# Attention heads of two kinds: one after the other, or in alternating pieces of two tiles

## The reference

```python
xn  = layernorm(x)
# attention 1 ("poly"): 16 heads of 128, rope on q and k
s   = (q1 @ k1.T) ** 4 * causal
o1  = (s @ v1) / max(s.sum(-1), 1e-6);  attn1 = o1 @ Wo1.T
# attention 2 ("sfmx"): 16 heads of 128 on h1 = rmsnorm(xn)
p   = softmax(causal(q2 @ k2.T / sqrt(128)))
attn2 = (p @ v2) @ Wo2.T;   mod = 0.1 * tanh(attn2 @ A)
# MLP on h = rmsnorm(xn)
g   = silu(h @ W_in.T + mod * (h @ A) @ B);  up = h @ W_up.T
out = x + attn1 + xn + (g * up) @ W_down.T
```

## Time and profile before

| | us |
|---|---|
| median of the runs (2: 8290.56 and 8651.73) | 8471.14 |
| the profiled execution | 7604.0 |
| its span, first to last instruction, slowest core | 7602.5 |
| spans of all cores | 7588.0 to 7602.5 |
| mean granted TensorE clock, all cores | 0.895 to 0.897 of full speed |

### The profile page before, as it was taken

One profiled execution on the slowest core, in us unless ns is written; L12 is line 12 of the kernel. 1 busy time (PEld: TensorE's weight loads), 2 busy tenths in 40 slices (PEclk: granted clock), 3 DMA queues, 4 the chain that ended last, 5 costly groups with the idle time before them and its releaser, 6 DMA issues.

```text
span 7602.5 us, 67624 instructions; the slowest of 8 cores (7588.0 to 7602.5 us)
## 1 busy us (share of the span) xinstructions
PE 5990.3 (79%) x25648; PEld 2466.4 (32%) x25648; DVE 1493.0 (20%) x1800; ACT 1372.8 (18%) x1974; POOL 823.5 (11%) x877
## 2 busy tenths in 40 slices
PE   3188885998666666666678858999999999679779
PEld 0033342444212121121223313444444444234334
DVE  3333302000223323233221121000000000111112
ACT  1011112111345454454520011000000000000000
POOL 0000000000242333424310000000000000000000
PEclk6699997999888887887789979999999999789889
DMA  4322232433101000010023141132231230686775
GB/s 84 122 64 61 61 61 39 77 75 63 43 25 34 25 25 25 26 34 25 25 48 96 25 86 45 34 67 55 46 67 42 59 67 12 176 216 189 201 193 186
DMA packets 285258, 552.72 MB, mean 73 GB/s; under 512 B 143879, under 2 KB 177031, under 8 KB 277511
## 3 DMA queue, kind: packets, MB, share of 16 engines
q0 software_dynamic: 60432, 310.72, 19.5%
q1 hardware_dynamic: 206078, 204.11, 8.5%
q10 hardware_dynamic: 18432, 33.56, 1.7%
HBM read 598.98 MB, written 125.85 MB: 95 GB/s over the span
## 4 chain that ended last, share of the span: by engine, by line
PE 70%; ACT 9%; DVE 8%; DMA 5%; issue 4%; POOL 3%; DVEq 1%; ACTq 0%; POOLq 0%; SPq 0%
PE big L360 18%; PE big L752 12%; PE big L826 12%; PE big L757 12%; PE big L612 6%; ACT px L543 4%; POOL px L538 3%; PE big L563 3%; PE big L568 3%; DMA pb<-gu_sp 2%; DVE px L553 2%; PE big L527 2%; DMA px<-xt 2%; ACT px L365 2%; PE big L762 1%
## 5 line engine op out<-in xcount | busy, mean ns | idle before, releaser
L752 PE MATMUL big<-pb 128*128 128x512 bf16 x4096 | 1556.8, 380 | 6.2 <-DVE px L725 6.2
L757 PE MATMUL big<-pb 128*128 128x512 bf16 x4096 | 1553.9, 379 | 0.0
L360 PE MATMUL big<-pb,px 128*128 128x512 bf16 x6144 | 1341.2, 380 | 260.2 <-DMA px<-ropes 185.8
L826 PE MATMUL big<-pb 128*128 128x512 bf16 x4096 | 892.8, 381 | 202.4 <-DMA pb<-gu_sp 202.4
L563 PE MATMUL big<-px 128*128 128x512 bf16 x1280 | 570.3, 446 | 568.9 <-DVE px L553 290.9
L360 PEld LDWEIGHTS big<-pb,px 128*128 128x128 bf16 x6144 | 600.9, 98 | 984.7 <-issue 270.2
L538 POOL TENSOR_TENSOR px<-px 128x512 bf16<-128x512 f32 x640 | 662.7, 1058 | 1238.8 <-ACT px L534 1163.4
L826 PEld LDWEIGHTS big<-pb 128*128 128x128 bf16 x4096 | 402.4, 98 | 693.9 <-issue 216.1
L568 PE MATMUL big<-px,ones 128*128 128x512 bf16 x1280 | 573.4, 448 | 0.0
L752 PEld LDWEIGHTS big<-pb 128*128 128x128 bf16 x4096 | 400.6, 98 | 519.1 <-issue 66.8
L757 PEld LDWEIGHTS big<-pb 128*128 128x128 bf16 x4096 | 401.4, 98 | 454.0 <-issue 1.6
(11 more groups left out here) (97 smaller groups left out, 2184.2 us busy)
## 6 DMA issues: line engine op xcount, KB each, us to landing
pb<-gu_sp POOLq DMA_DIRECT2D x32, 4096.0 KB, 19.6
pb<-wint POOLq DMA_DIRECT2D x16, 2048.0 KB, 15.9
pb<-wupt POOLq DMA_DIRECT2D x16, 2048.0 KB, 26.3
gu_sp<-px SPq DMA_DIRECT2D x64, 512.0 KB
pb<-wdnt POOLq DMA_DIRECT2D x8, 4096.0 KB, 29.9
px<-xt SPq DMA_DIRECT2D x32, 512.0 KB
q_sp<-px SPq DMA_DIRECT2D x32, 512.0 KB
k_sp<-px SPq DMA_DIRECT2D x32, 512.0 KB
```

The source lines that it names most:

```text
L360: e.matmul(PS(4 * bi + tb), wbuf[b][:, jc * 128:(jc + 1) * 128], src_pool[:, jc * NT + tb * 512: jc * NT + (tb + 1) * 512], start=(jc == 0 ...
L752: e.matmul(PS(gbk), winb[:, jc * FB + fc * 128: jc * FB + (fc + 1) * 128], PB1[:, jc * NT + tb * 512: jc * NT + (tb + 1) * 512], start=(jc ...
L757: e.matmul(PS(ubk), wupb[:, jc * FB + fc * 128: jc * FB + (fc + 1) * 128], PB1[:, jc * NT + tb * 512: jc * NT + (tb + 1) * 512], start=(jc ...
L826: e.matmul(PS(bk), PB2[:, fc * ICB + ici * 128: fc * ICB + (ici + 1) * 128], PB1[:, fc * 512:(fc + 1) * 512], start=(fc == 0), stop=last),
```

## The change

`attention_head` becomes a generator. Its first argument after the head is `sid`, 0 for poly and 1 for sfmx. It yields after its loads, after the norms of k, after those of q, after the bias, after every second tile (and the last, incomplete pair of the pipeline), and after each block's scaling. The loop over heads makes both generators and calls them in turn until both end, poly first. So on every engine pieces of the poly head stand between pieces of the sfmx head.

With it go: each kind has its own accumulator banks (4 and 5, or 6 and 7) for all blocks, its own two of the four score slots, and its own single `arm1` buffer. Within an iteration SV(t-2) and DN(t-2) now come ahead of QK(t). The norms use banks 6 and 7 in place of 4 and 5.

In the last stage `e1` and `e2` have one buffer each in place of two, and a DVE drain follows the sum.

```diff
-        def attention_head(kind, h, sh, q_sp, k_sp, v_sp, outF, bar):
-            b = sh % 2
-            w0 = list(bar) if sh < 2 else []
+        def attention_head(kind, h, sid, q_sp, k_sp, v_sp, outF, bar):
+            b = sid
+            w0 = list(bar)
+            sv_bk = 4 + 2 * sid
+            dn_bk = 5 + 2 * sid
...
+            yield
             t_negb = None
             if kind == "sfmx":
...
+                S.tc[("nsq",)] = tr
+                yield
+                tsq2 = S.op("dve", lambda e, b=b: e.tensor_tensor(out=aqsq[:], in0=aqh[b][:], in1=aqh[b][:],
+                                                                  op=ALU.mult),
+                            waits=[tq, tm], incs=[("dve", 1)])
...
+                S.tc[("aqsqpe",)] = tm
+                yield
...
+                yield
             for tqb in range(NTB):
-                sv_bk = 4 + 2 * (tqb % 2)
-                dn_bk = 5 + 2 * (tqb % 2)
                 for t_ in range(ntile + 2):
+                    if t_ >= 2:
+                        tt_ = t_ - 2
+                        sl2 = 2 * sid + tt_ % 2
...
                     if t_ < ntile:
-                        sl = t_ % 4
+                        sl = 2 * sid + t_ % 2
...
-                    if t_ >= 2:
-                        tt_ = t_ - 2
-                        sl2 = tt_ % 4
...
-                ab = (2 * sh + tqb) % 2
-                arm1 = arm1s[ab]
+                    if t_ % 2 == 1:
+                        yield
+                arm1 = arm1s[sid]
...
+                yield
...
         for h in range(H):
-            attention_head("poly", h, 2 * h, scr["q1_sp"], scr["k1_sp"], scr["v1_sp"], PB1, bar_p2a)
-            attention_head("sfmx", h, 2 * h + 1, scr["q2_sp"], scr["k2_sp"], scr["v2_sp"], PB2, bar_p2a)
+            bar_h = bar_p2a if h == 0 else []
+            ga = attention_head("poly", h, 0, scr["q1_sp"], scr["k1_sp"], scr["v1_sp"], PB1, bar_h)
+            gb = attention_head("sfmx", h, 1, scr["q2_sp"], scr["k2_sp"], scr["v2_sp"], PB2, bar_h)
+            a_done = b_done = False
+            while not (a_done and b_done):
+                if not a_done:
+                    try:
+                        next(ga)
+                    except StopIteration:
+                        a_done = True
...
-        e1s = [pxf(40, 512), pxf(0, 512)]
-        e2s = [pxf(42, 512), pxf(2, 512)]
+        e1 = pxf(40, 512)
+        e2 = pxf(42, 512)
...
+                               waits=[tlx, t_ar, t_mr, S.tc.get(("e1",))], incs=[("dve", 1)])
...
+                    S.op("dve", lambda e: e.drain())
+                    S.tc[("e2",)] = teo
...
-                    S.tc[("e1", eb)] = tst
+                    S.tc[("e1",)] = tst
```

More of the change, by code:

```diff
@@ new lines, in attention_head @@
+                tsq = S.op("dve", lambda e, b=b: e.tensor_tensor(out=aqsq[:], in0=akh[b][:], in1=akh[b][:],
+                                                                 op=ALU.mult),
+                           waits=[tk, S.tc.get(("aqsq",)), S.tc.get(("aqsqpe",))] + w0,
+                           incs=[("dve", 1)])
+                for qtr in range(NTB):
+                    nbk = sv_bk + qtr % 2
+                    tm = S.op("pe", lambda e, qtr=qtr, nbk=nbk: e.matmul(
+                              PS(nbk), ones128[:], aqsq[:, qtr * 512:(qtr + 1) * 512],
+                              start=True, stop=True),
+                              waits=[tsq, S.t_ps[nbk]], incs=[("pe", 1)])
+                    tr = S.op("dve", lambda e, qtr=qtr, nbk=nbk: e.reduce_max(
+                              out=nmax8[:, qtr:qtr + 1],
+                              in_=PS(nbk), axis=mybir.AxisListType.X),
+                              waits=[tm], incs=[("dve", 1)])
+                    set_ps([nbk], tr)
@@ new lines, in attention_head @@
+                S.tc[("nsq",)] = tr
+                yield
+                tsq2 = S.op("dve", lambda e, b=b: e.tensor_tensor(out=aqsq[:], in0=aqh[b][:], in1=aqh[b][:],
+                                                                  op=ALU.mult),
+                            waits=[tq, tm], incs=[("dve", 1)])
+                for qtr in range(NTB):
+                    nbk = sv_bk + qtr % 2
+                    tm = S.op("pe", lambda e, qtr=qtr, nbk=nbk: e.matmul(
+                              PS(nbk), ones128[:], aqsq[:, qtr * 512:(qtr + 1) * 512],
+                              start=True, stop=True),
+                              waits=[tsq2, S.t_ps[nbk]], incs=[("pe", 1)])
+                    tr = S.op("dve", lambda e, qtr=qtr, nbk=nbk: e.reduce_max(
+                              out=nmax8[:, 4 + qtr:4 + qtr + 1],
+                              in_=PS(nbk), axis=mybir.AxisListType.X),
+                              waits=[tm], incs=[("dve", 1)])
+                    set_ps([nbk], tr)
@@ L523, in attention_head @@
                 for t_ in range(ntile + 2):
+                    if t_ >= 2:
+                        tt_ = t_ - 2
+                        sl2 = 2 * sid + tt_ % 2
+                        S.op("pe", lambda e, sl2=sl2, tt_=tt_, b=b, sv_bk=sv_bk,
+                             st=(tt_ == 0), en=(tt_ == ntile - 1):
+                             e.matmul(PS(sv_bk), avh[b][:, tt_ * 128:(tt_ + 1) * 128],
+                                      as4[sl2][:], start=st, stop=en),
+                             waits=[t_w[tt_], tv] + ([S.t_ps[sv_bk]] if tt_ == 0 else []))
+                        tsv = S.op("pe", lambda e, sl2=sl2, tt_=tt_, dn_bk=dn_bk,
+                                   st=(tt_ == 0), en=(tt_ == ntile - 1):
+                                   e.matmul(PS(dn_bk), ones128[:], as4[sl2][:], start=st, stop=en),
+                                   waits=[S.t_ps[dn_bk]] if tt_ == 0 else [],
+                                   incs=[("pe", 1)])
+                        S.tc[("as4", sl2)] = tsv
                     if t_ < ntile:
-                        sl = t_ % 4
+                        sl = 2 * sid + t_ % 2
                         tqk = S.op("pe", lambda e, sl=sl, t_=t_, tqb=tqb, b=b:
@@ L583, in attention_head @@
                                out=arm1[:], in_=PS(dn_bk), func=AF.Ln),
-                               waits=[tsv, S.tc.get(("arm", ab))], incs=[("act", 1)])
+                               waits=[tsv, S.tc.get(("arm", sid))], incs=[("act", 1)])
                     set_ps([dn_bk], tln)
@@ L647, in build @@
         for h in range(H):
-            attention_head("poly", h, 2 * h, scr["q1_sp"], scr["k1_sp"], scr["v1_sp"], PB1, bar_p2a)
-            attention_head("sfmx", h, 2 * h + 1, scr["q2_sp"], scr["k2_sp"], scr["v2_sp"], PB2, bar_p2a)
+            bar_h = bar_p2a if h == 0 else []
[8 more added lines that the diff above has]
+                        a_done = True
+                if not b_done:
+                    try:
+                        next(gb)
+                    except StopIteration:
+                        b_done = True
         bar_attn = S.barrier()
@@ L861, in build @@
                     set_ps([bk], te2)
                     S.op("dve", lambda e: e.drain())
[L863 to L864 removed]
+                    teo = S.op("dve", lambda e: e.tensor_tensor(out=e1[:], in0=e1[:], in1=e2[:], op=ALU.add),
                                incs=[("dve", 1)])
[L866 removed]
```

37 lines of the change are left out of this document (8 added, 29 removed).

## The result

The changed kernel is faster: the ratio to the kernel before is 0.972, with a 95% interval from 0.967 to 0.977. Forecast was a ratio of 0.977 and, for an execution like the profiled one, 7429 us; the comparable executions of the changed kernel took 7417 to 7439 us, beside 7604 and 7665 before. The forecast of the median in absolute terms, 8276 us with a range from 8060 to 8600, was wrong: the median of 13 runs is 7650 us (7417 to 8336), and that of 10 runs of the kernel before is 8136 (7604 to 8652).

The account below looks back on a forecast made before the run. The attention stage was taken as bound by waits. A pair's terms, 33.9 + 51.2 + 15.3 + 6.3 + 1.9, made 108.6 us; 7604 - 178 + 3 = 7429 us, scaled to 8276 us, range 8060 to 8600.

Parts of the forecast that it names:

- The start-up: Start of each pair of heads, from the last sfmx scaling through loads, norms, bias and first exp: 33.9 us.
- turn 6: One of a pair's 32 turns, each a poly piece then an sfmx piece; its end closes the 33.9 us start.
- The turns: Poly's other tiles: ten turns without masks at 2.89 us and six masked at 3.72, 51.2 us a pair.
- Block ends: Three turns using poly's last tiles, each followed by one with its scaling: 3 x 5.1 = 15.3 us a pair.
- the sfmx head alone: End of a pair: one masked loop 2.3 us, 1.83 to the last SV, scaling 2.2: 6.3 us.
- The clock: Attention stage: PE dense after the start, one turn in sixteen at the lower level, 1.9 us a pair.
- The rivals that kept it low: Attention stage: today's clock share stays, 9.5 us a pair more, chance 0.12; low throughout, 129 us, chance 0.14.
- The port: Rival: six of sixteen sfmx masks beside POOL lose 0.88 us each, 5.3 us a pair, -1.2%; chance 0.15.
- The last stage: With a single buffer, each bank waits for the store, 1 us late; the last block's three followers add 3 us.
- The step that failed: Whole kernel: the ratio 0.977 from the profiled execution was carried to the runs' median, 8471 us, giving 8276 us.

Follow-up runs that it names:

- the streams: Changed kernel with loads and norms of heads 1 to 12 a head ahead, both kinds as endless streams, and QK ahead of SV: 7174 us.

## Why the prediction was right, and where it was wrong

**The start-up, 33.9 us: right in its chain, 2.3 too long.** Each of its marks lay within 0.5 us of the trace (6.9, 16.3, 25.1, 26.6 us). What made it work was to follow each engine's queue in order: the q squares behind the poly masks, the first exp behind the poly scaling. Its last piece, the 16 matmuls up to the end of turn 6, was 2 us too long, because the clock rose before I let it rise: matmuls are 0.43 us apart up to 2111.57 and 0.22 after it. The start-up took 31.6 us.

**The turns, 51.2 us: the loop right, the masks too cheap.** 2.95 us for 2.89, and for masked ones 4.1 in the mean for 3.72. The 0.3 us that I added for a mask beside POOL was the term too small: the mask meets the square in most turns, and then it costs 0.75 us (4.22 for 3.47). That the poly head alone has turns of 2.94 us shows that this is its own loop and not PE's, ACT's or POOL's load; the masks show the same, and putting QK first shows which link of it can be cut.

**Block ends, 15.3, and the sfmx head alone, 6.3: not read one by one.** Behind the start-up the pair took 76.3 us (107.9 for this pair, less 31.6). Mine was 74.7 (108.6 less 33.9). A masked turn with the block end behind it took 8.9 us twice, for 8.8. That the whole pair came out within 0.7 us is in part luck: the clock's early rise paid for the dear masks.

**The clock: right.** 0.96 after the start-up, 0.56 in it, with one turn of this pair at the lower level, as put down. The rivals that kept it low are out. (The sentence that no engine is busier than half the time holds for the engines beside PE; PE itself was busy 1211 of 1916 us.)

**The port: out where I had it, present where I hadn't.** All sfmx masks together cost 1 to 2 us a pair, and only 38 of the stage's 256 took over 0.9 us, 2.4 of sixteen where the rival had six. Of the 256 poly masks 90 did, and these stand in the loop that sets the turn. The exclusion that the Trainium skill states ("SBUF — State Buffer", section "SBUF: two separate sides") is visible in durations, here as before; the sfmx masks that lost by it had slack, the poly masks had none.

**The last stage, 3 us: wrong, it is 0.** I took the median time to landing of all 64 stores, 4.8 us. At the end the store and its handover take 2.3 to 2.4 us (3.0 to 3.3 now and then), and from the sum's start to the end of the subtraction 4.5 us pass, where the next bank is ready after 5.75 (7571.85 to 7577.60). The term was mis-sized by taking the median of the whole stage for its end; that the large loads of the stage make the difference is likely and not shown.

**The step that failed: from 7429 to 8276 us.** "The runs' median is 11% above the profiled execution and I can't say from one trace which part is longer, so I carry the ratio over." The two runs behind the median were 4% apart and both far above the trace, whose cores all agreed. That spread said that the median of two was no property of the kernel; 13 and 10 runs later the medians are 7650 and 8136, each set by how many of its executions were long: their ratio is 0.940, while that of the comparable executions, 0.972, is near the forecast. The range was built around that median with a scatter of 2% and so left out the profiled execution's own level, 7429, which was the only one with an explanation. It should have reached from it to the upper run.

**What the change leaves on the table** I hadn't asked. The order SV before QK, the two slots and the single pair of banks came along with the alternation and cost 25 us a pair where nothing alternates. In the alternation one move of a line gives back 9 us, starting the next head's loads and norms early 12.5, and both together 19.3 (107.2 to 87.9).

## What to carry to other kernels

When two streams alternate on an in-order engine, write down for each engine what stands in front of the first instruction of each piece: the turn is then the longest loop through one stream (here PE, ACT, POOL, PE), and the start of a stream is a chain that can be summed from a few rows. An alternation that halves the slots of each stream should be weighed with the matmul that consumes a slot behind the one that fills the next, not ahead of it. Of the absolute time, forecast the level of the profiled execution when all its cores agree, and take the spread of the runs as the range.

## What the runs showed of the hardware

The port between VectorE and GpSimd shows itself in an operation that the kernel before never ran beside POOL. The squares of k, 128x2048 bf16, take 1.22 us alone and 2.10 us in the streams, where they stand in the middle of a poly head; those of q, three pieces later, keep their 1.21 us (the two lines above). What decides is who starts first, in the first of the six pairs of squares:

```profile
2044.85 5.01 POOL L599 TENSOR_TENSOR px<-px 128x512 bf16<-128x512 f32 x4 [0.60 <-ACT px L595]
2044.87 2.10 DVE L487 TENSOR_TENSOR px<-pb 128x2048 bf16<-128x2048 bf16 x1
...
2055.81 1.21 DVE L507 TENSOR_TENSOR px<-pb 128x2048 bf16<-128x2048 bf16 x1
2056.26 2.65 POOL L599 TENSOR_TENSOR px<-px 128x512 bf16<-128x512 f32 x2 [1.86 <-ACT px L595]
```

The square of k starts 0.02 us after a POOL square and takes 0.88 us longer, which is under that square's 1.04, and the same in all six to within 4 ns. The next POOL square waits in its turn: the four take 5.01 us, where three took 3.03 in the earlier trace rows. The square of q starts 0.45 us before a POOL square, and there only POOL pays: its two squares take 2.65 us instead of 2.04. So it isn't a slowdown in proportion; the later one waits for the earlier one's end.

Second, a single core can't tell 10 us between two kernels here: in one execution of the changed kernel four cores of one die have attention stages of 1714 to 1734 us.
